# A two-layer graph kernel: edge fetches ahead of the y1 stores, y1 tiles in pairs, and another order of the last two y1 tiles

## What is computed

```python
h = maximum(layernorm(x), 0)
for Ws, Wn, b in ((Ws1, Wn1, b1), (Ws2, Wn2, b2)):
    h_neigh = segment_sum(h[src], dst, num_segments=1250)
    h = h @ Ws + h_neigh @ Wn + b
out = x + h
```

## Time and profile before

| | before |
|---|---|
| median of 3 runs | 735.92 us |
| the profiled execution's own time | 737.09 us |
| span of the profiled execution | 735.3 us |
| mean granted TensorE clock | 0.986 |
| PE busy | 682.8 us (93%) |
| DVE busy | 258.3 us (35%) |
| ACT busy | 131.3 us (18%) |
| POOL busy | 69.9 us (10%) |
| stage 1 ends, stage 2's first matmul | 207.57 us |

### The profile page before, as it was taken

The page is one execution under the profiler, slowest core; times in us unless marked ns, Lnnn a source line. Parts: engine busy times, 40 slices in busy tenths (PEclk is TensorE's granted clock), DMA queues, the critical chain, the costliest instruction groups (busy, mean ns, idle before and its releaser), DMA issues.

```text
span 735.3 us, 9034 instructions
## 1 busy us (share of the span) xinstructions
PE 682.8 (93%) x3400; PEld 579.6 (79%) x3400; DVE 258.3 (35%) x958; ACT 131.3 (18%) x218; POOL 69.9 (10%) x123
## 2 busy tenths in 40 slices
PE   2899949878879999999999999999999999999998
PEld 2688736666679999999999788688887788788885
DVE  4769999999810101010013611400001311300000
ACT  4461213112210212021114400300000201200000
POOL 5531114000000000000000000011110000111100
PEclk9999989999989999999999999999999999999999
DMA  7611241000122112121214000411112200411110
GB/s 247 195 38 38 53 107 69 30 29 30 47 61 63 30 38 61 30 62 35 63 29 135 29 0 1 143 44 44 57 58 94 85 0 0 157 43 57 57 54 27
DMA packets 48747, 44.83 MB, mean 61 GB/s; under 512 B 14993, under 2 KB 33435, under 8 KB 48710
## 3 DMA queue, kind: packets, MB, share of 16 engines
q1 hardware_dynamic: 48710, 44.37, 19.2%
HBM read 33.61 MB, written 10.74 MB: 60 GB/s over the span
## 4 chain that ended last, share of the span: by engine, by line
PE 73%; DVE 20%; DMA 3%; POOL 1%; issue 1%; ACT 1%; SPq 0%; DVEq 0%
PE PS L775 34%; PE PS L865 15%; PE PS L906 12%; PE PS L873 11%; DVE hot_n L666 9%; DVE hot_m L664 9%; DVE HT L724 1%; DMA W_raw<-ws_in 1%; DMA W_raw<-wn_in 1%; DMA xin<-x_in 1%; PE PS L802 1%; POOL W L411 1%; DVE W L707 0%; ACT W L467 0%; PE PS L767 0%
## 5 line engine op out<-in xcount | busy, mean ns | idle before, releaser
L775 PE MATMUL PS<-W,HT 128*128 128x512 f32 (+1 forms) x1440 | 352.5, 400 | 13.5 <-POOL W L411 10.3
L775 PEld LDWEIGHTS PS<-W,HT 128*128 128x128 f32 (+1 forms) x1440 | 265.8, 188 | 82.4 <-issue 8.3
L865 PE MATMUL PS<-HT,W_st 128*128 128x416 f32 (+1 forms) x576 | 113.6, 358 | 4.1 <-DVE W_st L713 4.1
L865 PEld LDWEIGHTS PS<-HT,W_st 128*128 128x128 f32 x576 | 110.6, 193 | 6.0 <-DVE W_st L713 4.6
L666 DVE TENSOR_SCALAR hot_n<-iota_n,window_edges 128x160 f16<-128x160 f16 x400 | 104.0, 260 | 0.0
L664 DVE TENSOR_SCALAR hot_m<-iota_m,window_edges 128x128 f16<-128x128 f16 x400 | 101.1, 253 | 1.6 <-PE PS L767 1.6
L906 PE MATMUL PS<-y,AT 128*128 128x512 f32 (+3 forms) x400 | 94.2, 390 | 0.0
L873 PE MATMUL PS<-AT,y_st 128*128 128x416 f32 (+2 forms) x480 | 93.5, 354 | 0.0
L873 PEld LDWEIGHTS PS<-AT,y_st 128*128 128x128 f32 (+1 forms) x480 | 90.9, 190 | 1.3
L906 PEld LDWEIGHTS PS<-y,AT 128*128 128x128 f32 (+3 forms) x400 | 74.1, 185 | 16.8
L458 POOL TENSOR_TENSOR x_out<-x_out,b_sb 128x512 f32<-128x512 f32 (+1 forms) x20 | 26.6, 1334 | 572.5 <-DMA x_out<-x_in 572.5
(11 more groups left out here) (60 smaller groups left out, 189.4 us busy)
## 6 DMA issues: line engine op xcount, KB each, us to landing
W_raw<-wn_in SPq DMA_DIRECT2D x32, 256.0 KB, 5.4
xin<-x_in SPq DMA_DIRECT2D x9, 512.0 KB, 9.2
y_dram<-y_out SPq DMA_DIRECT2D x18, 256.0 KB, 2.1
y_st_raw<-y_dram SPq DMA_DIRECT2D x8, 576.0 KB
x_out<-x_in SPq DMA_DIRECT2D x18, 256.0 KB, 2.6
out<-x_out SPq DMA_DIRECT2D x18, 256.0 KB, 2.0
W_st_raw<-ws_in SPq DMA_DIRECT2D x8, 512.0 KB, 3.9
W_raw<-ws_in SPq DMA_DIRECT2D x16, 256.0 KB, 4.1
```

Of the source, the lines that this page charges most:

```text
L775: ins = nc.tensor.matmul(PS[:r, bank, :], HT[:, a, k, t * P:t * P + r], W[:, k, b, :], start=first and m == 0, stop=last and m == 2)
L865: ins = nc.tensor.matmul(PS[:, banks[c], 0:w_], W_st[:, a, k, :], HT[:, b, k, o_:o_ + w_], start=k == 0 and m == 0, stop=False)
```

## The change

- `load_windows` 0 to 3 stand ahead of the first store; `load_windows(4 + i)` follows the store of tile i for i in 0 to 4, and `load_windows(9)` follows the last of these. None is left behind the stores of tiles 5 to 7.
- Tiles 8 and 9 are computed slab by slab in turn, and tiles 10 and 11 too. So the slabs of the second half are fetched from behind tile 7's store on.
- Tiles 18 and 19 begin with their slabs 5 and 6; then tile 18 ends, then tile 19. The wait for W_st's fetch is for slabs 5 and 6 alone, and `check` stands six slabs ahead of the end, which is right behind the last window of counts.

```diff
+def slab_sequence():
+    for i in (*range(EARLY, NT - 2), (NT - 2, NT - 1), (NT, NT + 1), *range(NT + 2, 2 * NT - 2)):
+        tiles = i if isinstance(i, tuple) else (i,)
+        yield from (("y1", tile, k) for k in range(KF) for tile in tiles)
+    a, b = 2 * NT - 2, 2 * NT - 1
+    yield from (("y1", i, k) for i in (a, b) for k in (5, 6))
+    yield from (("y1", i, k) for i in (a, b) for k in (7, 0, 1, 2, 3, 4))
+
+def first_slab(i):
+    return 5 if i >= 2 * NT - 2 else 0
+
+def last_slab(i):
+    return 4 if i >= 2 * NT - 2 else KF - 1
...
-    return order[:-2] + [("check",)] + order[-2:]
+    return order[:-6] + [("check",)] + order[-6:]
...
-        if event == ("y1", 2 * NT - 1, 7):
+        if event == ("y1", 2 * NT - 1, 6):
             yield ("w_st", 0)
...
-            for a in range(2):
+            for a in range(4):
                 load_windows(a)
...
             for i in range(EARLY):
                 save_y1(i)
-                load_windows(2 + i)
+                load_windows(4 + i)
+            load_windows(NT - 1)
...
-                    sp.wait_ge(w_used, KF - 1 + 3)
+                    sp.wait_ge(w_used, KF - 1 + 2)
                     load_w_st(0)
                 else:
                     save_y1(n)
-                    if n + 2 < NT:
-                        load_windows(n + 2)
...
-                    if i == 2 * NT - 1:
-                        y1_products(i, k, k == 5, k == 4)
-                    else:
-                        y1_products(i, k, k == 0, k == KF - 1)
+                    y1_products(i, k, k == first_slab(i), k == last_slab(i))
```

More of the change, by code:

```diff
@@ L61, in last_of_group @@
     return w % GROUP == GROUP - 1 or w == NW - 1
+def slab_sequence():
[9 more added lines that the diff above has]
+    return 4 if i >= 2 * NT - 2 else KF - 1
 def stage1_order():
-    slabs = [("y1", i, k) for i in range(EARLY, 2 * NT - 1) for k in range(KF)]
-    slabs += [("y1", 2 * NT - 1, k) for k in (5, 6, 7, 0, 1, 2, 3, 4)]
     order, w = [], 0
-    for n, slab in enumerate(slabs):
+    for n, slab in enumerate(slab_sequence()):
         order.append(slab)
```

## The result

The changed kernel takes 750.54 us (median of 4 runs, 749.34 to 751.54) and the kernel before 736.63 us (4 runs): a ratio of 1.0188, with a 95% interval of 1.0165 to 1.0211. It is 13.9 us slower. (The three runs of before that stood ahead of the prediction had a median of 735.92 us; a fourth, of 737.34, makes it 736.63.) The profiled execution took 749.83 us and its span is 748.0, so 12.7 us more than the span of before.

What follows compares the result with a forecast made beforehand. DVE was taken to bound stage 1b. DVE ending 17.5 us later, less 4.6 us at the end of stage 1, gave 12.9 us more on 735.92: 748.8 us, range 743 to 756.

Steps and rivals of the forecast that it cites:

- What bounds stage 1b: Stage 1b, 119.8 to 198 us: DVE's one-hots set the pace, 1.667 us a window, while PE waits for hot_n.
- The stores behind the fetches: SP's queue: tile 0's store moves from 44.82 to 59.1 us, tile 5's to 103.0, holding later tiles on PE.
- the first hold: Before tile 4: PE idles 7.3 us for tile 2's copy; DVE, its ring full, resumes at 75.4 instead of 65.45.
- DVE's end: End of DVE's stage 1b work: 17.8 us later from window 21's delay, less 0.3 for POOL's rebasings, so 17.5.
- The end of stage 1: Seam from last counts to stage 2: 2.0 us shorter, plus 2.6 from PE's clock staying up, 4.6 us less.
- Rival A: End of stage 1: holds are right but the seam gives nothing, 753.8 to 754.9 us; chance 16%.
- The pairs: Tiles 8 to 11: PE saves its 8.08 us wait, which lay beside DVE's work; costed at nothing.
- hold 2: Before tile 9: PE stands from 92.8 to 105.8 us for tile 5's store; window 21 begins at 108.7, not 90.9.
- B: Rival on the holds: only the one before tile 4 counts, 9.9 less 4.6 us, time 741.2 us; chance 7%.
- C: Rival on SP's queue: fetches under about 6 us, neither hold, seam's gain stays, 731.3 us; chance 6%.
- Rival D: Stage 1b: DVE doesn't bound after all, or the parts cancel; within 2.2 us of before; chance 2%.
- Rival E: After the hold before tile 9: PE stays behind DVE, slab casts ahead of copies on ACT; over 757 us; chance 4%.

Runs made afterwards that it cites:

- one hold alone: Changed kernel with fetches 8 and 9 put behind the stores of tiles 5 and 6, leaving only the hold before tile 4: 739.66 us, ratio 1.0046.
- the run with the second hold alone: Changed kernel with fetches 0 to 6 back among the stores, 7 to 9 still ahead of tile 5's store: 748.77 us, ratio 1.0175.
- The new end alone: Kernel before with only the order of the last two tiles, the earlier W_st fetch and the earlier check: 731.74 us, ratio 0.993.
- the run with the old fetches: Changed kernel with the fetches back where they were, keeping pairs and the order of the last two tiles: 733.38 us, ratio 0.9963.
- the best kernel: Kernel before with the new end, counts begun two slabs earlier and Wn1's second-half low parts made by DVE, not POOL: 727.88 us, ratio 0.9878.

## Why the prediction was right

748.8 us were forecast and 750.54 measured, inside the range of 743 to 756. By its own steps:

**What bounds stage 1b.** DVE does, with the ring of six windows as the only cover. A late DVE stayed late (one hold alone: 7.9 us at DVE's last one-hot, less the gain at the end, made 3.2), and a DVE shorter by 4.6 us brought 3.9, the rest being lost at check.

**The stores behind the fetches.** Forecast for tiles 0 and 5: 59.1 and 103.0; in the trace 58.17 and 102.76. Holds on PE: 7.3 and 13.0 forecast, 6.35 and 12.95 found. DVE resumed at 74.07 and 109.32 (75.4 and 108.7 forecast). That the second sets the end and the first is swallowed by it, the run with the second hold alone shows. That the stores were hit within 1 us is in part luck, as errors in SP's pace offset each other. From fetch to fetch without a store it was 6.8 us (7.15 forecast), and with one 7.67 (7.35 forecast). In the first hold the half clock was priced too high: 2.6 us for tile 4, where its 24 matmuls took 7.15 us, some 1.5 more than at full clock. The second hold made this harmless. "No hold" for tile 6 missed PE's 0.83 us, which didn't reach DVE.

**DVE's end.** Its last one-hot begins at 216.12, where it began at 197.98 before: 18.1 us later, 17.5 forecast. The difference is that of window 21, which began at 109.32 and not at 108.7: tile 9's two slabs before the counts took 2.7 us and not 2.5, and the counts behind them were slower than forecast (15 matmuls 2.22 us at half clock).

**The end of stage 1.** 2.0 us from a shorter path and 2.6 from the clock were forecast. The new end alone gave 5.0 us, of which its trace shows 1.8 and 2.4. In the changed kernel these two were 2.0 and 2.3 us. PE's branch did run beside its last slabs: it began at 219.4, and the slabs ended after 222. Rival A, which had this gain at nothing, fell. One of the signs was worked out wrongly: stage 2's first matmul was to be near 221, but the prediction's own sum gives 207.57 + 17.5 - 2.0 = 223.1. Measured were 223.80.

**The sum.** In the spans it was 18.1 - 2.0 - 2.3 us, and 1.2 less in stage 3, which no term had: 12.7, where 12.9 were forecast. DVE's 0.6 us more and these 1.2 us less worked against each other. In the medians it was 13.9.

**The pairs.** Costed at nothing, and nothing was measured for them alone, but the reason was incomplete. I had PE's 8.08 us disappear under DVE's cover; with the old fetches they only changed their releaser. In the changed kernel the pairs did cost something: they put tile 9, and so its wait for tile 5's store, ahead of counts that DVE's ring needs. That was in the sum, as hold 2.

**The rivals.** B had only the first hold count, at 741.2; the run with that hold alone took 739.66. C, without the holds but with the new end (731.3), is the run with the old fetches, 733.38; it needed the old order, since a fetch without a store took 6.8 us and not under 6. Rival D fell with the holds. Rival E, over 757 us, fell as well: from 120 to 216 us DVE worked without a break, so PE kept up with it.

**The one rule drawn on.** The Trainium skill, SBUF — State Buffer, section "SBUF: two separate sides", has a GpSimd operation and a two-port Vector operation exclude each other for the whole instruction. By it three rebasings moved into DVE's stands were to save nearly 3 us. In the trace only two begin inside DVE's waits, at 67.18 and 104.31, and their six operations of about 0.30 us would make nearly 2. DVE waited 18.45 us more than before (10.31 + 9.71 against 1.57) and ended 18.1 us later, so all the rest of its work together was only 0.3 us shorter. That is the 0.3 taken from the trace, and it does not bear the rule's size out for these small operations. For the slabs' low parts the trace agrees, with 1.34 instead of 0.25 us for an operation beside one, and the best kernel draws on that.

## What to carry to other kernels

In an in-order DMA queue, prefetches put ahead of stores delay whatever the stores free: ask of each store which buffer, which copy, which PSUM bank and at last which engine waits for it, and put numbers on the queue's pace (here 6.8 to 7.7 us for eight small fetches with register addresses) before moving anything. Two waits in a row on the path need not add up, so removing one may show little (1.8 us here, with the first hold gone). A wait on an engine that isn't the bound, as the 7 to 8 us on PE here, need not be on the path: the best kernel still has it. Put a flag that all engines branch on as early as its inputs allow, with independent work behind it: here PE's branch of 3.5 to 3.8 us then ran beside its last 18 matmuls.

## What the runs showed that I had not expected

- With pairs and the old fetches, ACT's in-order wait of 18.55 us for a slab that it need not have waited for yet passed PE's wait on to the counts (7.89 us): moving the use of a datum earlier in a hand-written order moves the casts too.
- In the changed kernel the busy times from 120 to 216 us show a mean clock of 0.98 and PE waited once 2.18 us for hot_n at 125.88, which cost nothing, as DVE was the bound there.
- Making the low parts on DVE and beginning the counts earlier took 4.6 us off DVE, as expected, but only 3.9 off the time, as check stayed where it was in PE's order and now stood behind two slabs. A kernel with check right behind the last count again was not run. One of the low parts waited 0.57 us for ACT's cast.
